# Value stage of a spectral-attention kernel: first loads in the score stage, and the sum of skip weights on TensorE

## The reference, cut to what matters

```python
x = x + _L0_conv_ref(_gn(x), ...)      # the layer of this change
x = x + _L1_conv_ref(_gn(x), ...)
# in the first layer
k = _fno_layer(xn, Kcw, Ksw, Hs, Ws)
q = _fno_layer(xn, Qcw, Qsw, Hs, Ws)
v = _fno_layer(xn, Vcw, Vsw, H, W)     # spectral_conv(xn, Vcw) + Vsw[n] * xn
scores = einsum('bntk,bnsk->bnts', qf, kf) / sqrt(Hs * Ws)
p_attn = softmax(scores, axis=-1)
av = einsum('bnts,bnsk->bntk', p_attn, vf)
p = _fno_layer(av, Pcw, Psw, H, W)     # spectral_conv(av, Pcw) + sum_n Psw[n] * av[n]
a = _inorm(p + xa, ...)
```

## Time and profile before

| | us |
|---|---|
| median of three runs | 1094.45 (1094.44 to 1097.9) |
| the profiled execution's own time | 1093.65 |
| its span | 1092.0 |
| VectorE has the probabilities | 182.12 |
| score stage, last operation | 189.42 |
| value stage, first product | 199.26 |
| value stage, last operation | 382.11 |

### The profile page before, as it was taken

The page is one execution under the profiler, slowest core; times in us unless marked ns, Lnnn a source line. Parts: engine busy times, 40 slices in busy tenths (PEclk is TensorE's granted clock), DMA queues, the critical chain, the costliest instruction groups (busy, mean ns, idle before and its releaser), DMA issues. The chain is left out here.

```text
span 1092.0 us, 36677 instructions
## 1 busy us (share of the span) xinstructions
PE 810.1 (74%) x16050; PEld 586.8 (54%) x16050; DVE 682.0 (62%) x1427; ACT 405.7 (37%) x882; POOL 365.4 (33%) x262
## 2 busy tenths in 40 slices
PE   0498493789999846999922899568767777776797
PEld 0365231222222216777712799457766666666686
DVE  4797597578888784555548899744444444443132
ACT  0297341123222263555533466423333333332121
POOL 0022471689999800111100000324444444442000
PEclk9999697699999967999965999888888888888899
DMA  9566710576464303334120776489999999998587
GB/s 363 113 186 153 163 27 3 185 292 196 165 198 168 108 0 95 95 83 141 49 90 7 192 192 191 106 191 252 270 266 264 264 263 264 263 264 188 156 261 212
DMA packets 270430, 189.36 MB, mean 173 GB/s; under 512 B 29108, under 2 KB 259221, under 8 KB 269269
## 3 DMA queue, kind: packets, MB, share of 16 engines
q1 hardware_dynamic: 189811, 131.47, 44.5%
q10 hardware_dynamic: 75426, 44.17, 16.6%
q0 software_dynamic: 5120, 12.75, 4.3%
HBM read 154.45 MB, written 33.07 MB: 172 GB/s over the span
## 5 line engine op out<-in xcount | busy, mean ns | idle before, releaser
L1960 PE MATMUL po<-pa,room 128*32 128x16 f32 x8320 | 146.8, 221 | 84.7 <-DMA room<-_L_conv_weight_imag_dram 59.3
L1960 PEld LDWEIGHTS po<-pa,room 128*32 128x32 f32 x8320 | 144.3, 162 | 92.5 <-issue 69.0
L979 POOL TENSOR_TENSOR q<-wb,xb 128x1536 f32<-128x1536 f32 (+1 forms) x51 | 170.2, 3364 | 41.0 <-DMA wb<-wv 33.3
L1049 DVE TENSOR_TENSOR q<-pw,xb 128x1536 f32<-128x1536 f32 (+1 forms) x85 | 140.7, 1702 | 25.0 <-PE acc L1019 13.7
L1019 PE MATMUL acc<-q,pt 128*32 128x384 f32 (+1 forms) x1088 | 103.7, 494 | 15.8 <-DVE q L1049 15.7
L2101 DVE TENSOR_TENSOR osl<-po,neg 128x128 f32<-128x128 f32 x64 | 18.3, 286 | 149.9 <-ACT neg L2034 149.9
L1913 POOL DMA_DIRECT2D os_<-osl x64 | 45.4, 713 | 182.7 <-DVE osl L2112 174.8
L1903 POOL COPY cols<-y 128x512 f32<-128x512 f32 x32 | 38.3, 1196 | 152.4 <-POOLq L1667 146.7
L2034 ACT ACTIVATE neg<-po 128x272 f32<-128x272 f32 x32 | 12.7, 397 | 197.0 <-issue 182.1
L1947 PE MATMUL px<-wbat,cols 128*32 128x130 f32 x2176 | 76.3, 292 | 4.2 <-DVE wbat L2072 3.0
L1019 PEld LDWEIGHTS acc<-q,pt 128*32 128x32 f32 x1088 | 27.7, 110 | 90.7 <-issue 55.1
(11 more groups left out here) (326 smaller groups left out, 1578.4 us busy)
## 6 DMA issues: line engine op xcount, KB each, us to landing
room<-_L_conv_weight_real_dram ACTq DMA_DIRECT2D x32, 520.0 KB, 9.7
room<-_L_conv_weight_imag_dram ACTq DMA_DIRECT2D x32, 520.0 KB, 12.7
room<-_L_conv_weight_real_dram SPq DMA_DIRECT2D x32, 520.0 KB, 7.0
room<-_L_conv_weight_imag_dram SPq DMA_DIRECT2D x32, 520.0 KB, 10.3
xb<-xns SPq DMA_DIRECT2D x64, 192.0 KB, 3.1
wb<-wv SPq DMA_DIRECT2D x16, 576.0 KB, 5.9
yall<-in_x_dram SPq DMA_DIRECT2D x4, 2048.0 KB, 14.6
xd<-in_x_dram SPq DMA_DIRECT2D x16, 512.0 KB, 4.2
```

The costliest lines, as they stand in the source:

```text
L979: nc.gpsimd.tensor_tensor(q2[:, t % 2, :, :, 0:m], bc(weights(blk, n), 2, NB), spectra(blk), ALU.mult).then_inc(s_qp, 1)
L1049: V.tensor_tensor(q1[:, t % 2, :, :, 0:m], bc(pw[t % 4][:, 0:3 * m].rearrange("p (r m) -> p r m", r=3), 2, NB), spectra(blk), ALU.mult).th ...
L1960: e = nc.tensor.matmul(po[u][32 * g:32 * g + 32, 512 * q + 16 * m:512 * q + 16 * m + 16], wsl[u][:, :, q * KWF + KWF - 1 - kw], xsl[u][:, ...
```

## The change

Five things are edited.

1. `vpb` and its two loads in the first stage go. In their place the score stage loads `Vsw` and `Psw` again (`vpc`) with a selection constant `dsel`, and VectorE makes from them, as the first thing of the stage, `vsel`: for each chunk a 128 x 32 matrix with the product of the two skip weights of head j where partition 4 s + j meets column s.
2. `selk` is loaded at the score stage's start.
3. `xr` and `xsum` lie in one region `lead`, which outlives the score stage; `wb` and `xb` are views of the same region. When the stores of the spectrum and of the weights have landed and the last region chunk is transposed, SyncE loads blocks 0 and 1 there, still in the score stage.
4. The transposed probabilities are copied in halves, by ScalarE and by VectorE, and with that the score stage ends.
5. The sum over heads is made by TensorE in the value stage, ahead of block 0: for each batch eight matmuls with `vsel` and `pt` add up in `pm[0]`; the transpose goes. VectorE copies the four results to `at` between its products 0 and 1 and makes `mt` and `cbeta` between products 1 and 2.

```diff
@@ first stage, ScalarE
-                    act.dma_start(rows[:, i, :], ...).then_inc(s_w, 16)
+                    if i < 2:
+                        act.dma_start(rows[:, i, :], ...).then_inc(s_w, 16)
@@ between the stages
+        vsel = att.enter_context(nc.sbuf_tensor("vsel", [128, NCK, NT], F32))
+        selk = att.enter_context(nc.sbuf_tensor("selk", [2 * NHD, NCK, 128], F32))
+        lead = att.enter_context(nc.sbuf_tensor("lead", [128, M2 + 2 * NUN * RH], F32))
+        wb = lead[:, 0:2 * NPL * 3 * MB].rearrange("p (u m) -> p u m", u=2)
+        xb = lead[:, 2 * NPL * 3 * MB:2 * (NPL + NB) * 3 * MB].rearrange("p (u m) -> p u m", u=2)
@@ score stage, SyncE
                 sp.dma_start(ny[:, :], c["ny"]).then_inc(s_wg, 16)
+                sp.dma_start(dsel[:, :], c["dsel"]).then_inc(s_vp, 16)
+                for i, n in enumerate(("Vsw", "Psw")):
+                    sp.dma_start(vpc[:, i, :], bass.AP(a["L0_conv_" + n].tensor, 0, [[0, 128], [1, NHD]])).then_inc(s_vp, 16)
+                for v in range(2):
+                    sp.dma_start(selk[NHD * v:NHD * v + NHD, :, :], ...).then_inc(s_sel, 16)
                 sp.wait_ge(s_xn, 1)
...
                 sp.wait_ge(s_wvs, 16 * (1 + 4 * NPL))
+                sp.wait_ge(s_r, 2 * NCH)
+                for blk in range(2):
+                    load_block(sp, blk)
@@ score stage, ScalarE
+                act.wait_ge(s_pt, 1)
+                act.activation(pt[:, 0:NCK // 2, :], psc[:, 0:512].rearrange("p (k i) -> p k i", i=NI), ACT.Copy)
@@ score stage, TensorE
-                m.then_inc(s_pt, 1)
-                pe.wait_ge(s_a, 1)
-                nc.tensor.transpose(tp[0][:, 0:NI], ad[:, :], ident[:, :]).then_inc(s_at, 1)
-                pe.wait_ge(s_atc, 1)
-                nc.tensor.matmul(tp[1][:, 0:1], at[:, :], v1("beta"), start=True, stop=True).then_inc(s_cb, 1)
+                    if k in (NCK // 2 - 1, NCK - 1):
+                        m.then_inc(s_pt, 1)
@@ score stage, VectorE
+                dve.wait_ge(s_vp, 48)
+                ch.link(V.tensor_tensor(vpc[:, 0, :], vpc[:, 0, :], vpc[:, 1, :], ALU.mult))
+                heads = vpc[:, 0, :].rearrange("p (k j) -> p k j", j=PB)
+                ch.link(V.tensor_tensor(heads, heads, bc(dsel[:, NT:NT + PB], 1, NCK), ALU.mult))
+                ch.link(V.reduce_sum(vp[:, :], heads, axis=AX.X))
+                V.tensor_tensor(vsel[:, :, :], bc(dsel[:, 0:NT], 1, NCK), bc(vp[:, :], 2, NT), ALU.mult)
                 dve.wait_ge(s_xt, 16 * NB)
...
-                ch.link(V.tensor_tensor(sco[:, :, :]..., by_head, bc(vpk, 3, NT), ALU.mult))
-                ch.link(V.reduce_sum(am[:, :], sco[:, :, :].rearrange("p n s -> p s n"), axis=AX.X))
-                ch.link(V.memset(ad[:, :], 0.0))
-                for b in range(NB):
-                    s = V.tensor_copy(ad[32 * b:32 * b + 32, 32 * b:32 * b + 32], am[32 * b:32 * b + 32, :])
-                s.then_inc(s_a, 1)
-                dve.wait_ge(s_pt, 1)
-                V.tensor_copy(pt[:, :, :], psc[:, :].rearrange("p (k i) -> p k i", k=NCK)).then_inc(s_ptc, 1)
...
+                dve.wait_ge(s_pt, 2)
+                V.tensor_copy(pt[:, NCK // 2:NCK, :], psc[:, 512:1024].rearrange("p (k i) -> p k i", i=NI))
@@ value stage, SyncE
-                for blk in range(NBLK):
+                for blk in range(2, NBLK):
@@ value stage, TensorE
                 for t in range(4):
                     spread(t)
+                for b in range(NB):
+                    i = slice(32 * b, 32 * b + 32)
+                    for k in range(NCK):
+                        m = nc.tensor.matmul(pm[0][i, i], vsel[:, k, :], pt[:, k, i], start=(k == 0), stop=(k == NCK - 1))
+                m.then_inc(s_am, 1)
...
+                        if blk == 0 and k == 1:
+                            pe.wait_ge(s_at, 1)
+                            nc.tensor.matmul(pm[1][:, 0:1], at[:, :], v1("beta"), start=True, stop=True).then_inc(s_cb, 1)
+                        if blk == 0 and k == MIX_AT[0]:
+                            pe.wait_ge(s_mt, 1)
@@ value stage, VectorE
+                def skip_mixing():
+                    dve.wait_ge(s_am, 1)
+                    for b in range(NB):
+                        i = slice(32 * b, 32 * b + 32)
+                        m = V.tensor_copy(at[i, i], pm[0][i, i])
+                    m.then_inc(s_at, 1)
+                def mixing_matrix():
+                    dve.wait_ge(s_at, 1)
+                    V.scalar_tensor_tensor(mt[:, :], at[:, :], v1("alpha"), ident[:, :], ALU.mult, ALU.add)
+                    dve.wait_ge(s_cb, 1)
+                    V.tensor_copy(v1("cbeta"), pm[1][:, 0:1]).then_inc(s_mt, 1)
...
+                        if t == 1:
+                            skip_mixing()
+                        if t == 2:
+                            mixing_matrix()
```

More of the change, by code:

```diff
@@ L62, in constants @@
     c["selk"] = (head[:, None, None] == (4 * np.arange(NCK)[:, None] + np.arange(128)[None, :] % 4)[None]).reshape(NHD, -1) * 1.0
+    part = np.arange(128)[:, None]
+    c["dsel"] = np.concatenate([part // PB == np.arange(NT)[None, :], part % PB == np.arange(PB)[None, :]], 1) * 1.0
     c["ones"] = np.ones((128, 128))
@@ L315, in build @@
             hs = sb("hs", [NHD, 4])
-            rows = sb("rows", [128, 4, NHD])
+            rows = sb("rows", [128, 2, NHD])
             symv = sb("symv", [2 * RH, 2 * KH])
@@ L405, in _ @@
                     act.dma_start(hs[:, i:i + 1], bass.AP(src.tensor, 0, [[1, NHD], [1, 1]])).then_inc(s_w, 16)
[L406 removed]
+                    if i < 2:
+                        act.dma_start(rows[:, i, :], bass.AP(src.tensor, 0, [[0, 128], [1, NHD]])).then_inc(s_w, 16)
                 for i, n in enumerate(("Kcw", "Qcw", "Vcw")):
@@ L616, in _ @@
                 ch.link(V.tensor_tensor(qkb[:, :], rows[:, 0, :], rows[:, 1, :], ALU.mult))
-                ch.link(V.tensor_tensor(vpb[:, :], rows[:, 2, :], rows[:, 3, :], ALU.mult))
                 dve.wait_ge(s_gt, 1)
@@ L1031, in _ @@
                 V = nc.vector
+                ch = Chain(dve, s_v3)
+                def skip_mixing():
+                    dve.wait_ge(s_am, 1)
+                    for b in range(NB):
+                        i = slice(32 * b, 32 * b + 32)
[6 more added lines that the diff above has]
+                    V.tensor_copy(v1("cbeta"), pm[1][:, 0:1]).then_inc(s_mt, 1)
                 def combine(blk):
```

61 lines of the change are left out of this document (23 added, 38 removed).

## The result

| | before | after |
|---|---|---|
| median of the runs, us | 1096.33 (6 runs) | 1088.31 (6 runs, 1085.84 to 1093.17) |
| ratio | | 0.9931, 95% interval 0.9905 to 0.9958 |
| the profiled execution: its own time, span | 1093.65, 1092.0 | 1093.17, 1091.5 |
| block 2's load issued (t2) | 210.88 | 205.49 |
| block 3's first product | 235.92 | 230.66 |

The kernel is 0.7% faster; a ratio of 1 lies outside the interval. The forecast was 1088.6, worked out from the median of three runs of before, 1094.45; with three runs more that median is 1096.33.

A forecast was written before the change was run, and what follows sets the result against it. Stages run in sequence: 17 us between probabilities and first product were the target, GpSimd's products bounding the unedited steady stage. -8.05 + 2.5 - 0.3 = -5.85 us on the median 1094.45 gave 1088.6 us, range 1085.2 to 1092.8.

The forecast's parts named there:

- Tail of the score stage: Behind the probabilities VectorE's work shrinks to half a copy; the stage ends at 184.85 instead of 189.42, -4.57 us.
- Early loads: Loads of blocks 0 and 1 run beside the softmax, there by 178 with 7 us to spare.
- Rival (e): The early loads are not there when the value stage opens at 185.4; at worst 1092.1 us; chance 0.04.
- Head of the score stage: VectorE first waits for three small loads and works on them: +2.5 us, bounds +1.9 and +2.9.
- The sum over heads: TensorE's 64 passes ahead of block 0 in the value stage take 4.9 us, bounds 1.1 and 9.7.
- Rival (c): Each pass of the sum waits until the one before is written: 14.1 us, total 1099.6 us; chance 0.05.
- The clock behind it: TensorE works unbroken from 185.4, clock up from about 195; low throughout, the shift of t2 is -6.3 us.
- t2: Value stage, block 0's products done and block 2's load issued: 202.83 against 210.88, -8.05 us.
- rival (d): GpSimd holds VectorE's mixing matrix step in the value stage for one product, 3.43 us: 1092.0 us; chance 0.06.
- t2 to block 3: Value stage: block 3 starts 25.0 us behind t2, bound by transfers of 7.0 MB at 280 GB/s.
- Sum: Whole kernel: t2's shift -8.05, score stage's head +2.5, first stage -0.3, together -5.85 us.
- The signs of being wrong: Wrong if block 3 starts by another distance from t2, or the stages behind 382 us change length.

The follow-up runs named there:

- e8: Changed kernel with the two loops of the sum over heads exchanged, chunk outside and batch inside; one run, no ratio given, the 64 passes took 1.08 us.
- e5: Changed kernel with VectorE's product 1 made ahead of the copies of the summed skip weights; 1084.24 us, ratio 0.9891 to the kernel before.
- e3: Changed kernel with the loads of blocks 0 and 1 back at the front of the value stage; 1089.9 us, ratio 0.9944 to the kernel before.
- e4: Changed kernel with the two 2.16 MB transfers cut into four pieces each, behind the loads of blocks 4 to 11; 1085.09 us, ratio 0.9895.
- e7: Changed kernel with the edits of e1, e4 and e5 at once; 1079.03 us, ratio 0.9835 to the kernel before.
- e10: e1 and e4 together, plus the sum ahead of block 0's chunk 7, first mixed tiles in block 1, mixing matrix from PSUM; 1080.5 us, ratio 0.9847.
- e2: Kernel before with only the early loads, the shared region and early selk, vector sum kept; 1088.21 us, ratio 0.9918.
- e6: Changed kernel with the 32 matmuls of the sum over heads made twice; one run, no ratio given, t2 moved 0.2 us.
- e1: Changed kernel with VectorE's small-load wait and four operations moved from the score stage's head to its wait for the exponentials; 1086.56 us, ratio 0.9918.

## Why the prediction was right, step by step

- **Tail of the score stage.** Predicted 2.73 us behind the probabilities, measured 2.76.
- **Early loads.** Predicted to be there with 7 us to spare. They went out from 168.26 on, 17.4 us ahead of the end of the probabilities, where the prediction had 17.5; by the time of day that is 3.7 later, as the probabilities are 3.6 later. The transfers ended before 180 and the value stage opened at 188.7. Rival (e) is out.
- **Head of the score stage.** Predicted +2.5, bounds 1.9 and 2.9; measured +3.2 (79.39 and 79.57 against 76.20 and 76.28). The spectrum is touched 13.3 us behind the first stage's end in both profiles, 10.7 and 10.3 in before's: 2.8. The other 0.4 was not in the sum. TensorE's clock rose 1.1 us later in the mean, counted from VectorE's first work on the spectrum, and the score loop's second step, first in before and then after, took 0.65 us more; that the 0.4 is this was not tested apart:

```profile
128.24 1.07 PE L802 MATMUL psc<-room,xrm 128*32 128x512 f32 x8
```

```profile
131.26 1.72 PE L829 MATMUL psc<-room,xrm 128*32 128x512 f32 x8
```

- **The sum over heads.** The largest term mis-sized: 4.9 taken, 2.88 measured, inside the bounds 1.1 and 9.7. The row nearest in shape, the transposes, was the wrong guide. The lower bound is real in the other loop order (e8, 1.08 us in four column groups); nothing came near the upper. Rival (c), full serialisation at 14.1 us, is refuted in its size, not in its kind.
- **The clock behind it.** I had it up from about 195. It rose at 194, TensorE then stood 2.02 us, and it was at half again from 197.5 to 204.3. I had taken TensorE as working without a break, though my own timetable has it through with product 0 about a microsecond before product 1 is made. From the end of product 1 to GpSimd's third product it took 4.92 us (197.09 to 202.01), not 3.0. This gave back 1.9 of the 2.0 us that the cheap sum had saved. e5 shows both together.
- **t2.** Predicted 20.7 us behind the probabilities, measured 19.8: the stage opened 0.2 nearer, GpSimd's third product came 0.3 nearer to its first, and VectorE's way, which was to end 0.4 last, did not. VectorE ended at 205.10, GpSimd's third product at 205.46, so GpSimd set it.
- **Mixing matrix, rival (d).** 0.34 us: GpSimd stood still then, as the timetable had it. e3 shows that the hold is real where they meet, 2.76 us.
- **t2 to block 3.** Predicted 25.0, measured 25.17 and 25.21, and between 24.5 and 26.1 in all kernels that issue the two large transfers behind block 2's load; 22.3 and 21.1 where they are spread (e4, e7), and 24.2 in e10, where TensorE holds GpSimd. It is transfer-bound. A block's loads are 1.38 MB (128 x 2688 numbers of four bytes), not the 1.34 that the prediction and e4's expectation have; the rate of that stretch is then 283 GB/s in place of 280, and nothing else changes.
- **First stage.** Predicted -0.3; the ends are 106.28 and 106.40 against 105.92 and 106.76, no difference that can be told.
- **Sum.** -5.85 predicted; measured -6.0 at the start of the last stage, by the means of two profiles each, and -7.6 and -7.5 by the times with 2.9 us of uncertainty either way. That the forecast fits to 0.3 us, 1088.6 and 1088.31, is luck twice over. In the front the errors of the sum and of the clock cancel, and that of the head was covered by t2. In the time the gain is 1.7 us larger than forecast, and the median of before, from which it was taken, 1.9 us higher than the three runs had it.
- **The signs of being wrong.** Block 3 did not start by another distance from t2. Of the stages behind, those up to the last kept their length (318.4 and 318.8 us in before, 318.0 and 318.1 after); the last was 3 to 5 us longer in both profiles of the changed kernel, which the times don't show.

What the prediction did not ask is whether both halves of the change pay. By the marks the loads alone (e2) are 3.8 us better, while the times of the two can't be told apart: moving the sum shortened the tail by 4.5, put as much between there and t2, and cost 3.2 at the head.

## What to carry to other kernels

When a transfer is moved out of a stage's front, look at what becomes first in line there: here a small sum and the order of two VectorE steps held back GpSimd, and swapping them was worth 2.9 us. Small loads that a stage needs late should not be waited for at its head. Price a change against its halves, and read the gain at marks: a run's time also holds clock phases of later stages (3.5 us in the stage itself here) that the edit only shifts.

## What the runs showed of the hardware that was not expected

- Passes of 32 weight columns and 32 moving columns, at half clock: 0.045 us each with eight matmuls in a row on one column group and one set of sums, 0.017 each when successive matmuls change the group (64 passes in 2.88 and 1.08 us). In the second case four passes start within 0.020 us.
- TensorE's clock rose at 194 after unbroken work from 188.7, TensorE stood 2.02 us soon after, and the clock was at half from 197.5 to 204.3. With 1.6 us more work ahead of the same gap (e6) it stayed full over it and read 0.69 in 198 to 202. In e1, with the same work, it did not rise before the gap at all.
- The same code with the same gap of 3.21 us at the inverse stage's opening ran at full clock in eight kernels, and at half for 6.8 or 10.2 us in four (before, changed, e2, e6); the gap began at most 5.62 us behind the clock's rise in the first case and at least 5.70 in the second.
- A VectorE step with two SBUF operands (128x128) took 2.76 us instead of 0.34 and ended with GpSimd's running product; four 32x32 steps with one operand in PSUM took 1.02 us at the same place.
